# Self-attention score maxima: each head's own 64 rows of the stacks, two heads in two row groups of the array

## The reference

```python
h1 = _ln(x, n1_g, n1_b)
x  = _attn(h1, h1, q1, k1, v1, o1_w, o1_b, 20) + x       # self-attention, 20 heads of 16
h2 = _ln(x, n2_g, n2_b)
x  = _attn(h2, context, q2, k2, v2, o2_w, o2_b, 20) + x  # attention over the 361 context rows
h3 = _ln(x, n3_g, n3_b)
a, g = split(h3 @ ff_w1 + ff_b1)
return (a * gelu(g)) @ ff_w2 + ff_b2 + x
# _attn: softmax(q @ k.T / 4) @ v for each head, then @ wo + bo
```

## Time and profile before

| | |
|---|---|
| runs, median (lowest to highest) | 1306.25 us (1305.75 to 1308.15) |
| the profiled execution: its time, its span | 1303.07 us, 1301.3 us |
| mean granted TensorE clock | 0.984 |
| PE, DVE, ACT, POOL busy of the span | 95%, 64%, 52%, 46% |
| weight loads (PEld) busy | 89% |

### The profile page before, as it was taken

How to read it: one execution, slowest core, us unless ns; L and a number is a source line. 1 busy time by engine, 2 the same in 40 slices (tenths; PEclk the granted TensorE clock), 3 DMA queues, 4 the chain that set the end, 5 groups by cost and what they waited for, 6 DMA issues and landing times. The chain is left out here.

```text
span 1301.3 us, 34279 instructions
## 1 busy us (share of the span) xinstructions
PE 1233.0 (95%) x12788; PEld 1154.2 (89%) x12788; DVE 828.6 (64%) x1606; ACT 672.3 (52%) x1622; POOL 603.2 (46%) x792
## 2 busy tenths in 40 slices
PE   5999869999999999999999999998799999999999
PEld 3899758999899998999999889996699999999999
DVE  5554457878888788788887888876565243342521
ACT  4565326666666666666666666664552322313131
POOL 5431125555555565554655555542664343423331
PEclk8999879999999999999999999999899999999999
DMA  4576654454545555455445454443121101010000
GB/s 128 195 237 219 210 150 131 144 164 131 165 142 162 180 152 172 157 161 184 128 149 160 130 160 138 149 134 87 37 65 38 36 6 46 0 50 0 25 1 26
DMA packets 105145, 154.49 MB, mean 119 GB/s; under 512 B 20780, under 2 KB 86564, under 8 KB 104996
## 3 DMA queue, kind: packets, MB, share of 16 engines
q1 hardware_dynamic: 104996, 152.49, 37.8%
HBM read 62.98 MB, written 28.93 MB: 71 GB/s over the span
## 5 line engine op out<-in xcount | busy, mean ns | idle before, releaser
L1418 ACT ACTIVATE probs<-expin 120x400 f32<-120x400 f32 (+2 forms) x635 | 297.7, 506 | 129.3 <-PE expin L811 125.5
L1095 DVE TENSOR_REDUCE neg_max<-score 100x2 f32<-100x722 f32 x320 | 287.9, 900 | 94.1 <-PE score L785 92.8
L811 PE MATMUL expin<-qs,ks 128*120 128x200 f32 (+2 forms) x1270 | 197.6, 269 | 3.5 <-ACT probs L1418 1.8
L811 PEld LDWEIGHTS expin<-qs,ks 128*120 128x120 f32 (+2 forms) x1270 | 176.3, 179 | 13.1 <-ACT probs L1418 7.9
L785 PE MATMUL score<-ks,qs 128*100 128x362 f32 x640 | 169.8, 347 | 18.4 <-DVE neg_max L174 11.6
L2657 DVE SCALAR_TENSOR_TENSOR hidden<-ps_a,b_cols,gelu 128x320 f32<-128x320 f32 x100 | 55.1, 551 | 165.3 <-PE ps_a L2581 165.2
L1609 POOL MEMSET qs<- 128x2400 f32 (+1 forms) x58 | 112.6, 1942 | 81.4 <-PE expin L811 81.4
L2819 POOL TENSOR_TENSOR hid_lo<-hidden,hid_hi 128x320 fp32r<-128x320 f32 x100 | 88.1, 881 | 121.9 <-ACT hid_hi L2727 121.6
L2739 ACT ACTIVATE gelu<-ps_g,b_cols 128x320 f32<-128x320 f32 x100 | 52.8, 528 | 137.0 <-PE ps_g L2581 137.0
L785 PEld LDWEIGHTS score<-ks,qs 128*100 128x100 f32 x640 | 86.9, 168 | 40.0 <-issue 28.9
L190 POOL TENSOR_TENSOR scaled_heads<-turned_heads,rden 128x320 f32<-128x320 f32 x63 | 48.0, 762 | 141.0 <-DVE rden L195 141.0
(11 more groups left out here) (222 smaller groups left out, 2949.8 us busy)
## 6 DMA issues: line engine op xcount, KB each, us to landing
ks<-kc_parts SPq DMA_DIRECT2D x96, 362.0 KB, 3.7
qk_dram<-qk_parts SPq DMA_DIRECT2D x32, 500.0 KB, 5.2
qs<-q_parts SPq DMA_DIRECT2D x192, 75.0 KB
ks<-qk_dram SPq DMA_DIRECT2D x96, 125.0 KB
ctx_raw<-in_ctxT SPq DMA_DIRECT2D x64, 180.5 KB
ks<-kc_parts SPq DMA_DIRECT2D x96, 90.5 KB, 2.7
qs<-qk_dram SPq DMA_DIRECT2D x64, 125.0 KB
v_dram<-v_rows SPq DMA_DIRECT2D x32, 132.8 KB
```

The source lines that it names most:

```text
L811: mm = pe.matmul(dst, ks[a][u][:, k_slot(c) if a == 2 else c, j0:j0 + n], qs[a][u][:, :, q_slot(c) if a == 2 else c, :], start=True, stop= ...
L1095: ins = nc.vector.tensor_reduce(dst, src, AX_X, ALU.max, negate=True)
L1418: nc.scalar.activation(probs[e % NPT][0:n, :], expin[e % 2][0:n, 0:HG * N], ACT.Exp, scale=SCALE)\
```

## The change

The loop over the chunks is now the outer one and the loop over the two heads the inner one, and each matmul takes only the 64 partitions of its own head from queries and keys. The number of matmuls, their columns, their outputs and the semaphores stay the same.

```diff
 def own_products(pe, banks, queries, keys, i):
-    for a in range(2):
-        for k in range(HP // 2):
-            c = HP // 2 * i + k
-            mm = pe.matmul(banks[0:N, a, k * N:(k + 1) * N], queries[:, a, c, :], keys[:, c, :], start=True, stop=True)
+    for k in range(HP // 2):
+        c = HP // 2 * i + k
+        for a in range(2):
+            half = slice(64 * a, 64 * a + 64)
+            mm = pe.matmul(banks[0:N, a, k * N:(k + 1) * N], queries[half, a, c, :], keys[half, c, :], start=True, stop=True)
     return mm
```

## The result

Over the runs of both kernels the change took the time from 1307.22 to 1298.68 us (medians of six): a ratio of 0.9934 with a 95% interval of 0.9913 to 0.9955. The same kernel, run again, gave 1296.08 us beside 1307.38 for the kernel before, a ratio of 0.9913 (0.9897 to 0.9930). It is 8.5 to 11.3 us faster by the medians, 5.9 to 13.5 by the two intervals; forecast were 11.0 us and 1295.2. The profiled execution took 1297.57 us, its span 1295.8.

The account below looks back on a forecast made before the run. PE was taken to set the 23.45 us period. 29 samples at 0.39 us give 11.3, plus 0.4 for early samples, less 0.7 for late DMAs: 11.0 off 1306.25, so 1295.2 us. Range 1287 to 1306.

Parts of the forecast that it names:

- Loads limit the block, and two row groups load at once: Blocks 0 and 1: a pair of loads and matmuls each 0.088 us, first to last start 0.40 instead of 0.75.
- Rival A: Blocks 0 and 1: loads run one after the other whichever rows they use; 0.49 us slower a sample, 1321; chance 0.13.
- rival B: Blocks 0 and 1: a group's next load waits for its matmul, 0.132 us a pair; time 1303; chance 0.10.
- A switch costs 0.09 us: Around blocks 0 and 1: each change of tiling mode costs 0.09 us; three are added a sample, 0.27.
- Rival D: Around blocks 0 and 1: switching costs less where both sides use all columns; saving 0.66 a sample, 1286; chance 0.04.
- The sum, 0.39 us a sample: Both blocks of a sample: 0.70 us saved, less 0.27 for switches and 0.04 for line 811's exposed load.
- What has to keep up: DVE reductions, line 785's wait and query DMAs should keep pace; DVE has 0.07 us left before block 0's reduction.
- The wait of line 786 on the reduction: PE behind block 1's reduction: the 0.40 us wait moves with the block's end, neither shrinking nor growing.
- The query DMAs: Cross queries issued by SP: mostly land in time, late ones now and then; 0.7 us taken off the whole saving.
- rival C: Periods: another chain, DVE before block 0 or query DMAs, binds; half or more gain lost, say 1302; chance 0.09.
- The lead-in: Samples 1 and 2, with sample 0 in the first stage: together 0 to 1.2 us of gain, 0.4 taken.
- Rival A's limit: Blocks 0 and 1: from 0.128 us between pairs on, loads in series decide; the gain only equals the switches' 0.31.

Follow-up runs that it names:

- the cross scores: Row groups of 64 rows for the cross scores too, against the changed kernel: 1333.03 us, ratio 1.0198 to the kernel before.
- one block alone: Two kernels with 64 rows in only one block of samples 1 to 31, against the changed kernel: block 1 1300.84 us (0.9957), block 0 1304.01 us (0.9976).
- order alone: Chunks in the outer loop and heads in the inner one, all 128 rows, against the kernel before: 1305.3 us, ratio 0.9996.

## Why the prediction was right
The time lay in the range, and the sign and the mechanism were as forecast. By its steps:

- **Loads limit the block, and two row groups load at once.** Right, down to the pattern: ten starts in 0.64-0.25 = 0.39 us, predicted 0.40, with the second pair 0.13 behind the first and the others 0.087 apart, predicted 0.134 and 0.088. Rival A (1321) would have shown 1.1 for the ten, rival B 0.79. The inference from column groups to row groups was not tested ahead of the result; it held. The rule of the Trainium skill that rival B goes by ("TensorE: Matmul & The Clock Gate", What overlaps and what doesn't), that a load overlaps with matmuls only of another row group, doesn't hold here: a load of 0.088 and its own group's matmul of 0.044 in series would put the pairs 0.132 apart.
- **A switch costs 0.09 us.** Right: 0.23 into block 0 where it was 0.14, and from block 0 to line 812 (476.24 less the last start, 475.67+0.64-0.25 = 476.06) 0.18. Of the four places that gave the price, one (line 833 to 811) had 0.12, which the prediction took down to 0.09. Rival D, which had it for nothing, is out by the same rows; the cross scores show what a switch costs when there is little between two.
- **The sum, 0.39 us a sample.** Right: 0.40 for the period quoted, 0.38 and 0.34 over the 28 periods of the two profiles, late DMAs included; with one block alone 23.17 and 23.30 us a period where 23.18 and 23.31 were expected.
- **What has to keep up.** DVE before the reduction of block 0: 0.07 us left was forecast, 0.06 measured. Before the second reduction 0.43 was forecast and 0.30 was left, still no limit. The wait of line 786 on the reduction stays, as said: 10.6 us in 26 times, 11.6 in 29 before. The query DMAs: I took 0.7 us off for late ones. The waits for them are 2.0, 3.1, 3.0 and 2.2 us in the four profiles with both blocks changed throughout the periods, against 0.3 before and 1.1 in order alone, so this term was too small by up to 2 us. It is rival C on a small scale: rival C had half the gain or more lost.
- **The lead-in.** 0.4 us of gain was assumed; the experiment without the change there shows none that can be told, so nothing measured bears this term out.
- **Rival A's limit.** The prediction says that the two blocks gain only the 0.31 of the switches from a distance of 0.128 us on. By its own terms, 0.134 + 3d + 0.006 = 0.595, that distance is 0.15. At the measured 0.087 it decides nothing.
- **What the sum left out.** The same code differs by 8 us from run to run (1294.59 to 1302.45 for the changed kernel). A part of that is the time at the lower clock in lead-in and tail, and the sum has no term for it: the tail lost 2 us in both profiles of the changed kernel. The mechanism is confirmed by the rows to a hundredth of a microsecond a period. That the whole came out near 11 us is a weaker test: each median is good to 2 to 3 us, the profiled pair gained 5.5 us, and the medians gained 8.5 and 11.3. So some of the closeness of the total is luck.

## What to carry to other kernels
Where matmuls have few columns (here 100: 0.044 us under a load of 0.088), the weight load sets the pace, and halving the rows makes it no shorter; two heads in two row groups double the pace because their loads and matmuls run at once. The price is the change of mode on either side, here 0.09 us each and an open load, so put enough work between two switches: ten short matmuls paid, two long ones (362 columns, 320 visits) cost 35 us over the kernel. Look first at what stands next to the block; where the mode changes anyway, half the price is gone.

## What the runs showed of the hardware that was not expected
TensorE does not keep the program's order between row groups. With five matmuls of one group ahead of five of the other, the sixth started 0.13 us after the first and before the third. The Trainium skill says the opposite in "TensorE: Matmul & The Clock Gate", What overlaps and what doesn't: matmuls start and end in the order of the program. The starts in the trace don't agree (line 169 at 503.07, line 166's third at 503.15). The last matmul of the program was still the last to start in every block of that profile, and the semaphore on it was all that the reader of both banks waited for; where one group has less work than the other, that would have to be looked at first. It also makes the order of a loop matter less than it seems: heads in the outer loop cost 0.13 us of a block's 0.35 against pairs, not the whole gain.
